# Splitting a unit's two pairs of first-pass score products around a second-pass product, in the long slots of a pixel-transformer kernel

## The reference, cut to what matters

```
for i in range(NL):                                   # NL = 6
    xn = _adaln(x, noise_emb, n1_w[i], n1_b[i])
    q, k, v = jnp.split(xn @ qkv_w[i].T, 3, axis=-1)
    x = x + _attn(_rope(q), _rope(k), v, src_mask) @ so_w[i].T
    xn = _adaln(x, noise_emb, n2_w[i], n2_b[i])
    q, k, v = xn @ cq_w[i].T, context @ ck_w[i].T, context @ cv_w[i].T
    x = x + _attn(_rope(q), _rope(k), v, ctx_mask) @ co_w[i].T
    xn = _adaln(x, noise_emb, n3_w[i], n3_b[i])
    x = x + (gelu(xn @ f1_w[i].T + f1_b[i]) @ f2_w[i].T + f2_b[i])

scores = einsum('bqhd,bkhd->bhqk', q, k) / sqrt(HD)   # inside _attn
w = softmax(scores);  out = einsum('bhqk,bkhd->bqhd', w, v)
```

## Time and profile before

| what | value |
|---|---|
| median of 3 runs | 3958.15 us (3956.56 to 3959.05) |
| the profiled execution, its own time | 3955.36 us |
| span of that execution's instructions | 3953.5 us |
| PE busy | 3715.1 us, 94% |
| DVE busy | 2797.2 us, 71% |
| ACT busy | 2504.4 us, 63% |
| one long slot, of which 22 | 90.36 us |

### The profile page before, as it was taken

How to read it: one execution, slowest core, us unless ns; L and a number is a source line. 1 busy time by engine, 2 the same in 40 slices (tenths; PEclk the granted TensorE clock), 3 DMA queues, 4 the chain that set the end, 5 groups by cost and what they waited for, 6 DMA issues and landing times. The chain is left out here.

```text
span 3953.5 us, 53043 instructions
## 1 busy us (share of the span) xinstructions
PE 3715.1 (94%) x19504; PEld 1677.8 (42%) x19504; DVE 2797.2 (71%) x4497; ACT 2504.4 (63%) x4213; POOL 1111.1 (28%) x998
## 2 busy tenths in 40 slices
PE   4999999999999999999999999999999999998568
PEld 1233454433455433345433345533345533344557
DVE  6788766788766688866688866688866688863322
ACT  1677766677765677766677666577666677656123
POOL 2233322233322232322232322233322233311324
PEclk7999999999999999999999999999999999999879
DMA  7566533366533366533365543366544356532145
GB/s 197 119 159 148 129 76 76 83 155 149 134 77 76 79 152 146 135 85 76 76 152 141 137 92 77 76 146 141 134 90 100 83 138 168 129 70 73 44 119 101
DMA packets 282259, 448.74 MB, mean 114 GB/s; under 512 B 50824, under 2 KB 190224, under 8 KB 281488
## 3 DMA queue, kind: packets, MB, share of 16 engines
q1 hardware_dynamic: 237328, 378.51, 40.1%
q0 software_dynamic: 44672, 66.83, 7.4%
HBM read 278.54 MB, written 170.15 MB: 113 GB/s over the span
## 5 line engine op out<-in xcount | busy, mean ns | idle before, releaser
L1197 ACT ACTIVATE prob<-ps 128x512 f32<-128x512 f32 x3072 | 1758.2, 595 | 1017.6 <-PE ps L1120 1008.2
L1380 DVE TENSOR_REDUCE negmax<-ps 128x2 f32<-128x1024 f32 x1536 | 1818.2, 1218 | 230.7 <-PE ps L1147 222.4
L1133 PE MATMUL psv<-prob,v 128*32 128x512 f32 x6144 | 820.1, 606 | 0.7 <-ACT prob L1197 0.7
L1120 PE MATMUL ps<-qstack,kstack 114*128 114x512 bf16 x1536 | 560.7, 386 | 19.9 <-ACT prob L1197 14.7
L1120 PE MATMUL ps<-xin,zrow 114*128 114x512 bf16 x1536 | 561.1, 387 | 8.8 <-ACT prob L1197 4.1
L1120 PEld LDWEIGHTS ps<-qstack,kstack 114*128 114x128 bf16 x1536 | 141.1, 96 | 570.1 <-ACT prob L1197 398.9
L1095 PE MATMUL side<-nT,wf 128*128 128x256 f32 x1480 | 359.5, 386 | 21.8 <-DVE hT L1480 21.8
L1120 PEld LDWEIGHTS ps<-xin,zrow 114*128 114x128 bf16 x1536 | 141.4, 96 | 558.0 <-ACT prob L1197 386.2
L1106 PE MATMUL side<-wf,hT 128*128 128x256 f32 x1456 | 329.3, 379 | 0.0
L1480 DVE TENSOR_SCALAR hT<-side,f1b 128x256 f32<-128x256 f32 x370 | 161.4, 478 | 211.3 <-PE side L1095 210.7
L1095 PEld LDWEIGHTS side<-nT,wf 128*128 128x128 f32 x1480 | 274.8, 191 | 75.4 <-DVE hT L1480 39.2
(11 more groups left out here) (260 smaller groups left out, 3943.2 us busy)
## 6 DMA issues: line engine op xcount, KB each, us to landing
bounce<-parts SPq DMA_DIRECT2D x288, 256.0 KB, 2.5
value_sums<-osum SPq DMA_DIRECT2D x192, 256.0 KB, 6.8
xin<-bounce SPq DMA_DIRECT2D x192, 192.0 KB, 6.0
zrow<-bounce SPq DMA_DIRECT2D x192, 192.0 KB, 6.5
qstack<-bounce SPq DMA_DIRECT2D x192, 192.0 KB, 5.7
kstack<-bounce SPq DMA_DIRECT2D x192, 192.0 KB, 6.3
bounce<-low SPq DMA_DIRECT2D x96, 256.0 KB, 2.1
hT<-value_sums POOLq DMA_DIRECT2D x94, 256.0 KB, 5.1
```

Source lines behind the costliest of these rows:

```text
L1120: nc.tensor.matmul(ps2[:, n % RING2, :], kk[0:ROWS, h, kt * P:(kt + 1) * P], q[0:ROWS, h, :], start=True, stop=True).then_inc(s_p2full, 1)
L1133: mm = nc.tensor.matmul(psv[32 * i:32 * i + 32, 0, :], v[j % 2][:, kt, (HD + 1) * h:(HD + 1) * h + 32], prob[:, 4 * (u % 2) + i, :], start ...
L1197: nc.scalar.activation(prob[:, 4 * (u % 2) + i, :], ps2[:, n % RING2, :], ACT.Exp, scale=HD ** -0.5).then_inc(s_prob, 1)
L1380: nc.vector.tensor_reduce(out_at, ps1[:, 2 * (n % 2):2 * (n % 2) + 2, :], AX, ALU.max, negate=True).then_inc(s_p1free, 1)
```

## The change

In the long slots a unit's second first-pass step moves behind P2(1): the queue of PE had P2(0), P1a, P1b, P2(1), side work, and now has P2(0), P1a, P2(1), P1b, side work. Short slots keep their order. No other engine's queue changes, no instruction is added or taken away, and every wait stays with its instruction.

```
                     if p1:
                         pass1(k, 2 * u)
+
+                    if p1 and not is_ffn(k):
                         pass1(k, 2 * u + 1)
                     if p2:
                         pass2(k - 1, u, 1)
+                    if p1 and is_ffn(k):
+                        pass1(k, 2 * u + 1)
                     for chunk in plan[2 * u]:
                         side_work(*chunk)
```

## The result

| | before | after |
|---|---|---|
| median | 3958.6 us (3956.56 to 3959.35, 4 runs) | 4039.15 us (4038.76 to 4039.99, 4 runs) |
| ratio after to before | | 1.0205, 95% interval 1.0187 to 1.0222 |
| span of the profiled execution | 3953.5 us | 4037.4 us |
| a long slot (slot 24) | 90.36 us | 94.16 us |
| a short slot (slot 27) | 58.9 us | 58.9 us |

The forecast was 4035 us, in a range from 4000 to 4060. The long slots carry the loss: 94.16 - 90.36 = 3.80 us, times 22 = 83.6, beside 83.9 between the two spans. The 22 together grew by 85.3, and what lies outside them was 1.4 us shorter.

What follows compares the result with a forecast made beforehand. PE's queue was taken to bound the long slots. Ordinary units 1.54, units where P2(1) can't come earlier 1.47 and waiting units 0.58 gave 3.59 us per slot, times 22 = 79.0 us; forecast 4035 us, range 4000 to 4060.

Steps and rivals of the forecast that it cites:

- What bounds: Long slots: PE, busy 87.81 of 90.36 us, sets the slot; other engines matter only where PE waits for them.
- Price of a change of shape: PE between whole-array and half-array products: about 0.10 us each, four instead of two per unit; +0.19 in an ordinary unit.
- The late second f32 record: Side-work chunk directly behind a first-pass pair: its second f32 record comes later, +0.10 us, lower bound 0.
- The held units: Units 0, 2, 8, 12: P2(1) waits for an exponential, starts no earlier, second pair now comes behind it; 1.47 us a slot.
- the wait in unit 12: Second feed-forward chunk's 0.97 us wait for DVE, which reads the first chunk: moves with that chunk and hides nothing.
- unit 8's shift: P2(2), with no chunk ahead, stands 0.63 instead of 0.49 us behind P2(1): +0.14, carried on through ACT's exponentials.
- The wait in unit 8: PE's idle time for ACT before the second set of transposes: should still be about 1.07 us after the change.
- Waits that hide: Units 4, 7, 9, 10, 11, 13: the longer way to the side work eats existing waits, leaving 0.58 us per long slot.
- The smaller loss: Rival, chance 0.14: long chunks' second record not late and P2(1) not held by an exponential; 1.79 us a slot, 3998 us.
- the larger one: Rival, chance 0.11: no wait of today hides anything in the long slots; about 4.97 us a slot, 4067 us.
- the faster one: Rival, chance 0.03: long slots wait for ACT, so exponentials 0.22 us earlier gain unit 8's 1.07 us wait; 3935 us.
- the move is free: Rival, chance 0.04: PE places P2(1)'s operand while the pair ahead streams, so shape changes cost nothing; no change, 3958 us.

## Why the prediction was right

- *What bounds.* PE's queue in the long slots, read by the distances between its starts: shown. Short slots did not move.
- *Price of a change of shape.* About 0.10 each, two more in a unit: shown by four distances of 0.32, by the run in which P2 has the pair's shape (no loss in ordinary units), and by the run with one change less (0.10 back in units that wait for nothing).
- *The late second f32 record.* It was taken over from slot 0, and it is there in every ordinary unit, 1.13 against 1.03; the run with the pairs together shows it nearly alone.
- *The held units.* P2(1) starts 0.05 behind the exponential's end in unit 12, and undoing the four units gives 1.50 us a slot where I had 1.47. That the wait in unit 12 moves with the chunk, and that unit 8's shift goes on through ACT, came out as well. The wait in unit 8 that I named as a sign did not stay at 1.07: the first set of transposes waited for DVE, which I had not counted, and the unit's sum is the same without it.
- *Waits that hide.* 0.66 us a slot measured alone, 0.58 forecast.
- *Sizes.* The forecast was 4 us low. A long slot grew by 3.80 us and not 3.59, 4.6 us in 22 slots. The 0.21 is spread over the units, 0.01 to 0.03 each: distances of 0.31 became 0.32 where the array has just changed its shape, and unit 3's transposes have a late second record too, which I had left out. The 3 us that I took off for a 0.31 in place of 0.32 from a pair to P2 went the wrong way: that distance was 0.32.
- *The rivals.* The smaller loss fell with the held units and the second record; the larger one with the waits; the faster one with unit 8, whose wait for ACT grew. That a pair's operand is put in place under the running product, so that the move is free, is refuted for the single pair as well, at 0.32 against 0.22. The rows of PE's weight loads (PEld) in unit 1 show it directly. Before, the loads of both pairs are over at 1798.50, 0.12 before the second pair starts (1798.62). After, the load of P2(1) begins with its product (1836.89 and 1836.90), and so does that of the second pair (1837.21 and 1837.22):

```profile
1798.39 0.11 PEld L1147 LDWEIGHTS ps<-zrow,xin 49*128 49x128 bf16 x4 [0.42 <-DVE negmax L1380]
...
1836.89 0.10 PEld L1120 LDWEIGHTS ps<-qstack,kstack 114*128 114x128 bf16 x1 [0.23 <-issue]
1837.21 0.10 PEld L1147 LDWEIGHTS ps<-zrow,xin 49*128 49x128 bf16 x2 [0.23 <-issue]
```

Of the two rules of the Trainium skill, the one in "TensorEngine Tiling (Array Packing)", "Key Properties" (changing the mode drains the engine), is what the trace agrees with, at 0.32 against 0.22. Whether the 0.10 us is such an emptying of the array or just the load itself, which lasts 0.10 in these rows, no run here separates.

## What to carry to other kernels

Where a matrix engine's queue sets the time, read the cost of an order from the distances between starts for each kind of neighbour, then count neighbours: here going between whole-array and half-array products cost 0.1 us each way, and a queue of 19504 instructions lost 2% by one order and won 0.4% by another, for the greater part by that; the rest were waits that the order made longer or shorter. Ask of every instruction that is moved forward what it waits for: one that cannot start earlier pushes the work it passed out of a gap that was free. Here it paid to put products of one small shape side by side, next to those of another small shape: a change from small to small costs no more than one back to the whole array, and saves the return.

## What was not expected

The granted clock fell in unit 9 of slots 23 and 33 in the changed kernel's profile, to 1.2 GHz from 2.4. In the profile of before it fell inside a long slot only in slot 47, behind a wait of 3.22 us for DVE in unit 5, and there it fell after the change too. Slot 23, PE's timeline, and the granted clock of the stretch (0.79):

```profile
1780.12 0.66 PE L1002 MATMUL side<-ident,hT 128*128 128x128 f32 x4 [1.24 <-ACT nT L1224]
...
1781.89 3.54 PE L1095 MATMUL side<-nT,wf 128*128 128x256 f32 x8
```

```profile
1780.60:1788.70 8.10, 8.10 (x35) 4.55 (x33) 3.23 (x4) 3.89 (x6) 4.63 (x3) 0.79 0.18 65
```

Eight feed-forward records took 3.54 us and not 1.99, and each of the two units was 1.69 us longer than its fellows. What PE did just before was to idle 1.24 us for ACT in unit 8, where before it idled 1.07; 19 other long slots have the same wait, 1.23 to 1.25 us, and no fall, and slot 47 waits 1.41 us there in both profiles, also without a fall in unit 9. Whether that idle time is the cause was not tried. The two falls are 3.4 of the 83.9 us between the spans.
